# Adaptive-norm block: pairs formed through PSUM, the gate for four chunks at once, more fillers at the end, second norm's statistics on VectorE

## What is computed

```python
h = layernorm(x) * (1 + ca) + sa            # ca, sa, ga, ...: per batch element, from c
q, v = relu(h @ enc_q), relu(h @ enc_v)      # 8 heads of 16
for each head:
    dist = sqrt(sum_e m * (q[window] - q)**2 + 1e-8)   # the 64 tokens up to this one
    keep the 32 nearest of the 64; infl = exp(-dist), normalised
    context = sum over the kept of infl * v
    gate = |q| > 0.2
    out = q * (context + gate * 0.1 * (q / |q|) @ (hebb_U @ hebb_V))
x = x + ga * (out @ decoder)
h = layernorm(x) * (1 + cb) + sb             # the second norm
x = x + gb * (h + routed experts(h))         # expert gates from token 0
```

## Time and profile before

| | |
|---|---|
| three runs | 719.01, 722.64, 726.97 us, median 722.64 |
| profiled execution | 718.8 us, its span 717.0 us |
| mean granted TensorE clock | 0.947 |
| busy: PE, DVE, ACT, POOL | 616.5, 645.2, 559.8, 510.4 us |

### The profile page before, as it was taken

The page is one execution under the profiler, slowest core; times in us unless marked ns, Lnnn a source line. Parts: engine busy times, 40 slices in busy tenths (PEclk is TensorE's granted clock), DMA queues, the critical chain, the costliest instruction groups (busy, mean ns, idle before and its releaser), DMA issues. The chain is left out here.

```text
span 717.0 us, 22533 instructions
## 1 busy us (share of the span) xinstructions
PE 616.5 (86%) x6006; PEld 435.1 (61%) x6069; DVE 645.2 (90%) x4890; ACT 559.8 (78%) x1734; POOL 510.4 (71%) x813
## 2 busy tenths in 40 slices
PE   4987889888889888888888888899888888888776
PEld 3544446666666666666666666666666666666554
DVE  5884698999999999999999999999999999999930
ACT  2895145888888888888888888888888888888753
POOL 3011437888888888888888888888888888888651
PEclk9996587999999999999999999999999999999965
DMA  6320000000000000000000000000000000000000
GB/s 203 88 61 4 10 16 18 21 26 25 26 21 26 23 26 25 26 25 25 26 26 25 25 26 25 22 26 23 25 25 27 25 26 25 26 24 24 16 5 16
DMA packets 41183, 21.22 MB, mean 30 GB/s; under 512 B 6040, under 2 KB 40544, under 8 KB 41056
## 3 DMA queue, kind: packets, MB, share of 16 engines
q1 hardware_dynamic: 41056, 19.77, 9.7%
HBM read 10.44 MB, written 4.19 MB: 20 GB/s over the span
## 5 line engine op out<-in xcount | busy, mean ns | idle before, releaser
L989 DVE MAX8 top<-modn_all 128x8 f32<-128x32 f32 x2048 | 201.7, 175 | 0.0
L558 POOL TENSOR_TENSOR big<-big,con 128x512 f32<-128x512 f32 x128 | 160.0, 1272 | 26.7 <-DVE big L1041 26.7
L995 DVE MATCH_REPLACE8 modn_all<-top,modn_all 128x32 f32<-128x32 f32 x1024 | 166.5, 174 | 0.0
L1218 PE MATMUL psC<-vst,big 128*128 128x68 f32 x512 | 105.1, 288 | 47.8 <-POOL big L558 47.8
L1218 PEld LDWEIGHTS psC<-vst,big 128*128 128x128 f32 x512 | 80.1, 197 | 70.6 <-POOL big L558 70.1
L1219 PE MATMUL psC<-vst,big 128*128 128x68 f32 x512 | 101.7, 281 | 0.0
L1219 PEld LDWEIGHTS psC<-vst,big 128*128 128x128 f32 x512 | 80.6, 199 | 0.0
L995 DVE MATCH_VALUE_LOAD modn_all<-top,modn_all 128x8 f32 x1024 | 77.9, 76 | 0.0
L499 POOL TENSOR_TENSOR wmod_sb<-key,meet 128x512 f32<-128x512 f32 x64 | 67.9, 1062 | 7.4 <-PE psX L1174 7.4
L544 POOL TENSOR_TENSOR t<-cst,rden 128x128 f32<-128x128 f32 x64 | 25.8, 403 | 63.8 <-DVE rden L1030 63.8
L700 ACT ACTIVATE cst<-psC 64x136 f32<-64x136 f32 x128 | 35.6, 278 | 38.3 <-PE psC L1219 36.8
(11 more groups left out here) (214 smaller groups left out, 1630.7 us busy)
## 6 DMA issues: line engine op xcount, KB each, us to landing
tst<-qT_all SPq DMA_DIRECT2D x256, 17.0 KB
big<-in_x SPq DMA_DIRECT2D x16, 256.0 KB, 2.8
xs<-in_x SPq DMA_DIRECT2D x64, 64.0 KB, 1.9
out<-yo SPq DMA_DIRECT2D x64, 64.0 KB, 1.6
sst<-nst SPq DMA_DIRECT2D x128, 3.0 KB
tst<-nst SPq DMA_DIRECT2D x128, 2.0 KB
con<-in_consts SPq DMA_DIRECT2D x1, 581.5 KB, 6.0
wmod_sb<-in_wmod SPq DMA_DIRECT2D x1, 384.0 KB, 4.6
```

The lines of the kernel that those rows point to most:

```text
L558: nc.gpsimd.tensor_tensor(wab[:, k % 2, v].rearrange("p (r t) -> p r t", r=4), wsel.rearrange("p (r t) -> p r t", r=4), part.unsqueeze(1). ...
L989: last = v.max(top[:, u, h, where], low_high[:, u, h])
L995: last = v.match_replace(low_high[:, u, h], top[:, u, h, 1:9], low_high[:, u, h], GONE)
L1218: mm(o, wab[:, k % 2, 0, cols], vst[:, blk + 1:blk + 3, r], start=True, stop=False)
```

## The change

Four edits. (1) The two reductions go. ScalarE writes the upper half of `key`, negated, into free columns of `psD` (`pHi`), and VectorE forms both halves of the pairs by scalar_tensor_tensor from `key` and `pHi` (`pairs`), for chunk i+1 at the end of step i, ahead of the scan. `pHigh` is written by ScalarE too. (2) The mean and variance of the second norm come from bn_stats and bn_aggr on VectorE; what ScalarE still does of it stands at the head of the next step. (3) `lnn`, `rnn`, `gat` and `hsc` are formed for four chunks at once, in every fourth step. (4) The counts of the fillers depend on the step in the last seven, and `drained` adds some in `psD` there. The diff, cut to its core (left out: allocations, semaphores, the indexing of `n2`, and the renumbering of `mix_step`), 8 columns to the left:

```diff
@@ -226,6 +225,7 @@
...
 pQH = pH[:, :, QH0:B0]
+pHi = pH[:, :, PW:PW + HW]
@@ -521,32 +524,33 @@
...
-        k = i + 1
-        if there(k):
-            pool.wait_ge(n2_ready, k + 1)
-            need(pool, mix_step, 4 * (k - 4) + 1)
-            nc.gpsimd.tensor_scalar(gat[:, k % 4], n2[:, k % 4], GATE2, 0.1, ALU.is_gt, ALU.mult).then_inc(gat_ready, 1)
+        if there(i - 2) and i % 4 == 2:
+            four = (i - 2) // 4
+            pool.wait_ge(n2_ready, 4 * four + 4)
+            need(pool, hsc_ready, four)
+            nc.gpsimd.tensor_scalar(gat[:], n2[:, four % 2], GATE2, 0.1, ALU.is_gt, ALU.mult).then_inc(gat_ready, 1)
+            pool.wait_ge(gat_ready, four + 1)
+            pool.wait_ge(rnn_ready, four + 1)
+            need(pool, mix_step, 3 * (i - 2))
+            nc.gpsimd.tensor_tensor(hsc[:], gat[:], rnn[:], ALU.mult).then_inc(hsc_ready, 1)
...
-            pool.wait_ge(rnn_ready, k + 1)
-            pool.wait_ge(gat_ready, k + 1)
-            need(pool, mix_step, 4 * k)
-            nc.gpsimd.tensor_tensor(hsc[:], gat[:, s4], rnn[:, s], ALU.mult).then_inc(mix_step, 1)
-            pool.wait_ge(mix_step, 4 * k + 1)
-            nc.gpsimd.tensor_tensor(t2[:].rearrange(h3, h=NH), hb, hsc[:].unsqueeze(2).broadcast_to([P, NH, HD]),
-                                    ALU.mult).then_inc(mix_step, 1)
+            pool.wait_ge(hsc_ready, k // 4 + 1)
+            need(pool, mix_step, 3 * k)
+            nc.gpsimd.tensor_tensor(t2[:].rearrange(h3, h=NH), hb, hsc[:, k % 4 * NH:(k % 4 + 1) * NH].unsqueeze(2)
+                                    .broadcast_to([P, NH, HD]), ALU.mult).then_inc(mix_step, 1)
@@ -672,18 +676,30 @@
...
-        k = i - 1
-        if there(k):
-            act.wait_ge(n2_ready, k + 1)
-            need(act, mix_step, 4 * (k - 2) + 1)
-            need(act, rnn_ready, k)
-            nc.scalar.activation(lnn[:], n2[:, k % 4], ACT.Ln, bias=bias[:, 6:7]).then_inc(lnn_done, 1)
-            act.wait_ge(lnn_done, k + 1)
-            nc.scalar.activation(rnn[:, k % 2], lnn[:], ACT.Exp, scale=-0.5).then_inc(rnn_ready, 1)
+        k = i - 4
+        if there(k):
+            s = k % 2
+            act.wait_ge(mvc_ready, k + 1)
+            need(act, nc_ready, k - 1)
+            need(act, rs_done, k)
+            nc.scalar.activation(lv_c[:], mv_c[:, s, 1:2], ACT.Ln, bias=bias[:, 0:1]).then_inc(lnc_done, 1)
+            nc.scalar.activation(nm_c[:, s:s + 1], mv_c[:, s, 0:1], ACT.Copy, scale=-1.0).then_inc(nm_done, 1)
+            act.wait_ge(lnc_done, k + 1)
+            nc.scalar.activation(rs_c[:, s:s + 1], lv_c[:], ACT.Exp, scale=-0.5).then_inc(rs_done, 1)
+
+        if there(i - 2) and i % 4 == 2:
+            four = (i - 2) // 4
+            act.wait_ge(n2_ready, 4 * four + 4)
+            need(act, rnn_ready, four)
+            nc.scalar.activation(lnn[:], n2[:, four % 2], ACT.Ln, bias=bias[:, 6:7]).then_inc(lnn_done, 1)
+            act.wait_ge(lnn_done, four + 1)
+            need(act, hsc_ready, four)
+            nc.scalar.activation(rnn[:], lnn[:], ACT.Exp, scale=-0.5).then_inc(rnn_ready, 1)
 
         k = i + 1
         if there(k):
             act.wait_ge(dist_ready, k + 1)
+            need(act, pair_done, 2 * k)
@@ -741,23 +758,18 @@
...
-            need(act, rs_done, k)
-            nc.scalar.activation(x2[:, s], pAtt, ACT.Copy, accum_out=sum_c[:]).then_inc(x2_ready, 1)
-            act.wait_ge(x2_ready, k + 1)
-            nc.scalar.activation(nm_c[:, s:s + 1], sum_c[:], ACT.Copy, scale=-1.0 / D).then_inc(nm_done, 1)
-            act.wait_ge(nm_done, k + 1)
-            nc.scalar.activation(dev_c[:], x2[:, s], ACT.Square, bias=nm_c[:, s:s + 1],
-                                 accum_out=ssq_c[:]).then_inc(ssq_done, 1)
-            act.wait_ge(ssq_done, k + 1)
-            nc.scalar.activation(lv_c[:], ssq_c[:], ACT.Ln, bias=bias[:, 0:1], scale=1.0 / D).then_inc(lnc_done, 1)
-            act.wait_ge(lnc_done, k + 1)
-            nc.scalar.activation(rs_c[:, s:s + 1], lv_c[:], ACT.Exp, scale=-0.5).then_inc(rs_done, 1)
+            nc.scalar.activation(x2[:, k % 2], pAtt, ACT.Copy).then_inc(x2_ready, 1)
...
         k = i + 1
         if there(k):
+            act.wait_ge(d2_ready, k + 1)
+            act.wait_ge(dist_ready, min(k + 2, NCH))
+            need(act, pair_done, 2 * k)
+            high = key[:, k % 2].rearrange("p (h u j) -> p h u j", h=NH, u=2)[:, :, 1]
+            nc.scalar.activation(pHi, high, ACT.Copy, scale=-1.0).then_inc(hi_ready, 1)
+
             e = infl[:, k % 2]
@@ -766,6 +778,14 @@
...
+
+        if there(i):
+            act.wait_ge(picked, 6 * i + 6)
+            need(act, w_ready, i)
+            if i == 0:
+                act.wait_ge(top_set, 2)
+            nc.scalar.activation(pHigh, top[:, 1].rearrange("p h n -> p (h n)"), ACT.Copy,
+                                 scale=-1.0).then_inc(high_done, 1)
@@ -995,14 +1015,21 @@
...
+    def pairs(k):
+
+        lo = key[:, k % 2].rearrange("p (h u j) -> p h u j", h=NH, u=2)[:, :, 0]
+        dve.wait_ge(hi_ready, k + 1)
+        need(dve, picked, 6 * k - 1)
+        v.scalar_tensor_tensor(out=low_high[:, 0], in0=pHi, scalar=-1.0, in1=lo, op0=ALU.mult,
+                               op1=ALU.min).then_inc(pair_done, 1)
+        need(dve, picked, 6 * k)
+        v.scalar_tensor_tensor(out=low_high[:, 1], in0=lo, scalar=-1.0, in1=pHi, op0=ALU.mult,
+                               op1=ALU.min).then_inc(pair_done, 1)
+
     def step(i):
         if there(i):
-            x4 = key[:, i % 2].rearrange("p (h u j) -> p h j u", h=NH, u=2)
-            dve.wait_ge(d2_ready, i + 1)
+            dve.wait_ge(pair_done, 2 * i + 1)
             need(dve, theta_ready, i)
-            v.tensor_reduce(low_high[:, 0], x4, AX_X, ALU.min).then_inc(pair_done, 1)
-            v.tensor_reduce(low_high[:, 1], x4, AX_X, ALU.max, negate=True).then_inc(pair_done, 1)
-            dve.wait_ge(pair_done, 2 * i + 1)
@@ -1045,16 +1072,25 @@
...
+        k = i - 3
+        if there(k):
+            dve.wait_ge(x2_ready, k + 1)
+            need(dve, mvc_ready, k)
+            v.bn_stats(st_c[:], x2[:, k % 2]).then_inc(stc_ready, 1)
+
         if there(i):
             dve.wait_ge(picked, 6 * i + 4)
             pick(1, 1)
 
+        if there(k):
+            dve.wait_ge(stc_ready, k + 1)
+            need(dve, nc_ready, k - 1)
+            v.bn_aggr(mv_c[:, k % 2], st_c[:]).then_inc(mvc_ready, 1)
+
+        if there(i + 1):
+            pairs(i + 1)
+
         if there(i):
-            dve.wait_ge(picked, 6 * i + 6)
-            need(dve, w_ready, i)
-            if i == 0:
-                dve.wait_ge(top_set, 2)
-            v.tensor_scalar(pHigh, top[:, 1].rearrange("p h n -> p (h n)"), -1.0, None, ALU.mult).then_inc(high_done, 1)
             dve.wait_ge(high_done, i + 1)
             need(dve, diff_ready, i - 1)
             v.tensor_tensor_scan(meet[:, i % 2].rearrange("p h n -> p (h n)"), pHigh,
@@ -1202,6 +1238,12 @@
...
+    def drained(times):
+
+        if times:
+            pe.wait_ge(pair_done, 2 * NCH)
+            keep_clock(psD[:, 0], PW, times)
...
             need(pe, cst_ready, 2 * k)
-            keep_clock(psC, PW, 3)
+            keep_clock(psC, PW, {NCH: 0, NCH + 1: 9}.get(i, 3))
...
+        drained({NCH - 1: 3, NCH: 3}.get(i, 0))
...
+        drained({NCH + 2: 2, NCH + 3: 6}.get(i, 0))
...
+            keep_clock(psX, PW, {NCH - 3: 3, NCH - 2: 4, NCH - 1: 3}.get(i, 0))
...
+        drained({NCH + 2: 3, NCH + 3: 2}.get(i, 0))
...
-            keep_clock(psX[:, 2 * P:4 * P], P, 2)
+            keep_clock(psX[:, 2 * P:4 * P], P, {NCH - 2: 6, NCH - 1: 5, NCH: 3, NCH + 1: 7}.get(i, 2))
```

32 lines of the change are left out of this document (17 added, 15 removed).

## The result

The changed kernel takes 686.73 us (median of 4 runs, 686.03 to 695.29), the kernel before in the same comparison 720.83 (4 runs, 718.79 to 726.97). The ratio is 0.954, 95% interval 0.944 to 0.964. The profiled execution has a span of 685.2 us against 717.0.

A forecast was written before the change was run, and what follows sets the result against it. VectorE, busy 90% of the span, was taken as the bound, its 9.29 us step falling to 8.75. Span 717.0 + 7.5 (head) - 34.2 (62 steps) - 7 (tail) = 683.3 us, so 689 us as median; range 676 to 706.

The forecast's parts named there:

- head: The first steps, up to scan 1, get longer because the pairs wait for pHi: +7.5 us, bounds +5 and +10.
- tail: From the last scan to the end, 45 more filler matmuls keep TensorE's clock: -7 us, bounds -9.5 and 0.
- VectorE's row: VectorE's own work in a step: 9.29 - 1.21 - 0.34 + 0.67 + 0.29 = 8.70 us.
- an idle of 0 to 0.1 before the scan: Sign on VectorE in the middle of the run: it waits only that long, in us, for ScalarE's pHigh.
- The loop: Two steps, from W through transposes, Ln, Exp, pHigh and scan back to a W: 8.72 us a step.
- the gate's delay: On ScalarE in every fourth step, lnn and its Exp: at most 0.6 us, 0.15 a step, taken as 0.03.
- the next step is shorter by VectorE's own: The step from scan 0 to scan 1 shrinks by 0.9 us, so scan 1 comes 7.5 later, not 8.4.
- the rival that it falls: TensorE's clock falls in the tail despite the new fillers: +10, 699 us; chance 0.14.
- Everything fits: Rival: 8.65 us a step, head +5, tail -9, giving 678 us; chance 0.09.
- The loop of 9.0: Rival: ScalarE comes 0.5 late to pHigh, once in two steps, so 9.0 us a step: 704 us; chance 0.12.
- the clock in the middle of the run: Rival: TensorE's clock falls there too, each such step costing 11.3 us, 766 us if in half; chance 0.03.
- pairs that wait: Rival: on VectorE the pairs wait 0.54 us for ScalarE in each step, giving 722 us; chance 0.02.

The follow-up runs named there:

- e3: The changed kernel with the two reductions of before in place of the pairs, and no pHi on ScalarE; 699.17 us.
- e10: e7 with the gate's Ln and Exp for four chunks moved on ScalarE to behind x2 of the step before; 668.51 us.
- e2: The changed kernel with pHigh negated on VectorE again, ahead of the scan; 690.96 us.
- e8: The changed kernel with three unread one-column copies on ScalarE between the last picks and pHigh; 702.06 us.
- e5: The changed kernel with the gate of before, 8 columns wide in each step on ScalarE and GpSimd; 696.75 us.
- e7: The changed kernel with pHigh between the influences' Ln and Exp on ScalarE, not behind the Exp; 672.18 us.
- e4: The changed kernel with the second norm's statistics on ScalarE as before, bn_stats and bn_aggr gone; 706.38 us.
- e9: The changed kernel with pHigh(0) ahead of pHi(1) on ScalarE and scan 0 ahead of the pairs of chunk 1 on VectorE; 685.42 us.
- e11: e10 without the fillers that the change added in steps 61 and 62; those from step 63 on stay; 668.55 us.
- e6: The changed kernel with one and one filler matmuls in place of three and two in steps 6 to 60; 686.16 us.

## Why the prediction was right, and where it was not

The time was right, 689 forecast and 686.7 measured, and so were the three parts of the sum: head +7.5 forecast and +6.8 measured (with a start 1.8 earlier), 62 steps -34.2 and -31.8, tail -7 and -6.8. The reasons are right in part. The head's number owes something to chance: counted from the distances of chunk 1 it costs 8.6, and the earlier start hides 1.8 of it.

**VectorE's row** was mis-sized: 8.70 forecast, 8.46 in e3 and e10, 8.48 in e2. Two of its terms are too high. The statistics were put at 0.29; they cost 0.16. The sixteen picks behind W took 1.61 (416.60 to 418.21), and picks and statistics together now take 1.77 (404.17 to 405.94): the picks are two times eight, of 0.75, and bn_stats stands between them, where 1.61 - 2 x 0.75 = 0.11 used to be idle. The pairs were put at 0.67 and take 0.64. Most of the rest, 0.08, lies between `den` and the instruction behind it, which forms the second half of `key`: some 0.25 before and 0.19 now. So VectorE idles 8.73 - 8.46 = 0.27 a step for pHigh, and the sign "an idle of 0 to 0.1 before the scan" was missed.

**The loop** had the right length, 8.72 for 8.73, and the wrong course. The step "(11.91 + 5.53) / 2" closes it through W and VectorE over two steps. The chain that the runs show has one step, and doesn't pass through W: Ln, Exp, pHigh, scan, GpSimd's difference, `key`, `cst`, `fst`, the counts, the distances, the transposes, Ln. The prediction names most of them, but not `cst`, `fst` and the counts, which close it. It set the gate's delay to almost nothing "since the relu behind them has to wait for GpSimd's difference in any case": that wait is 0.18, and the gate is 0.47, so 0.28 of it shows. A delay of ScalarE ahead of `fst` is paid in each step and not in every second one: e8 shows it, 0.25 a step where two steps would give 0.14, and e5 and e7 fit; e4's 9.055 fits both loops. That both loops give the same number is chance. One term stands in no row of the kernel before: Ln 0.05 behind the transposes, where those rows have 417.03 and 417.20. The changed kernel has 0.05 (405.41, 405.46).

**Where the negations stand.** The Trainium skill (ScalarE: Activation LUTs, Rules for kernel authors) would keep them on VectorE. Measured, pHigh on ScalarE behind the Exp gains 0.07 a step (e2 against the change), ahead of the Exp 0.28 (e2 against e7's mean of 8.52). The rows spoke against the rule and were right for pHigh (the place of pHi was not varied alone); more than the engine, it is the place in its queue that counts.

**The pairs never wait,** as forecast, in the usual steps: L1023 and L1026 last 0.39 and 0.41. The cover is smaller than the 1.1 forecast: pHi ends 1.8 after W (405.38), 0.56 ahead of the pairs. The wait of 0.78 ahead of C went to 0.2 and 0, as forecast.

**The head.** The products start 2.6 after the distances of chunk 1 (forecast 2.5), take 1.2 each, and the expert matmuls come 1.9 later than before, counted the same way (forecast 2.4). Scan 0 came at 105.13 + 1.8 = 106.9 (forecast 106.8). The step that failed is "the next step is shorter by VectorE's own": it took 12.21 as before (12.18), with 1.28 of wait for pHigh. Two things hold scan 0: pHigh(0), and the pairs of chunk 1 ahead of it, which need pHi(1). Both stand on ScalarE behind `nst`, which waits 10.6 for matmuls that TensorE does behind the expert products. Counted from the distances of chunk 1, scan 1 comes 31.6 later; without pHi (e3) it is 29.1, with pHigh on VectorE (e2) 30.0, with pHigh ahead of the Exp (e7) 29.6, in the order of e9 30.1. So each takes 1.5 to 2.6 of the 8.6 away, while the other hold stays; e3's 2.6 contain the 1.9 of the expert matmuls, which start 3.2 after the distances there, as in the kernel before. No run lifts both holds, so that the other 6 hang on them is argued from the rows and not shown.

**The tail.** The clock holds, the rival that it falls is refuted. But the prediction's -7 is not what the fillers are worth. Without them the tail is 28.4 and not 30.35, and the last scan comes 1.7 to 2.9 earlier. The fillers' own part is -2 to -3, too little for the medians. The prediction costed them as standing in waits; in steps 61 to 63 they stand in TensorE's row. That -7 and -6.8 agree is chance too.

**The rivals.** "Everything fits" (8.65 a step) falls for this kernel, and e10 at 8.46 shows that only ScalarE's order stood in its way. The loop of 9.0, the clock in the middle of the run, and pairs that wait are refuted by the rows above.

## What to carry to other kernels

Ask of a loop not only how long it is but how many steps it spans, and test it: put a known delay on one member and see whether each step pays all of it or half; measure the delay in the trace of that run, since mine was half of what I had planned. When an engine is no longer the bound, its small instructions can go where another engine's queue has a gap: the same two instructions of the gate cost 0.28 us in their step ahead of what TensorE waits for (0.35 in e7) and nothing in front of a wait (e10). Fillers that hold a clock belong where the engine waits; in a full row they cost time, here 1.2 us for those of two steps (e11 against e10).

## What the runs showed of the hardware that I had not expected

The time at which the clock comes back after the first steps is not a property of the kernel. The changed kernel and e6 are the same program up to step 5, but steps 2 and 3 took 10.23 and 8.52 in the one and 13.22 and 13.49 in the other. Windows of the changed kernel, then of e6:

```profile
125.00:145.00 20.00, 17.99 (x210) 12.49 (x197) 18.97 (x164) 15.57 (x44) 16.50 (x21) 1.00 0.07 19
```

```profile
125.00:145.00 20.00, 19.34 (x142) 12.80 (x144) 12.02 (x93) 9.78 (x27) 9.29 (x11) 0.57 0.05 13
```

At the granted clock of 0.57 two steps cost 8 us more (the step before them took 1.0 less). The single runs of 695.29 (changed), 693.5 (e6), 676.69 (e11) and 679.61 (e7) have the lowest mean clocks of their kernels (0.943 to 0.951), so this is likely much of the spread that hides 1 us; only the profiled ones among them (e6, e11) show the slow steps. The start differs too: the distances of chunk 1 began at 85.38 in e10 and at 89.28 in e11, with the same program ahead of them.

The two products of 1024 elements took 2.73 us each beside GpSimd's own and take 1.2 alone (2.35 for both, above); in e3, where they stand beside GpSimd's again, they take 2.03 each. GpSimd's two took 4.73 beside them, in the kernel before and in e3, and 3.75 in the changed kernel. Also, L1003 with 512 elements took 1.13 while GpSimd's L502 ran (105.72, 1.06 long) and 0.69 otherwise. The Trainium skill (SBUF — State Buffer, SBUF: two separate sides) has a VectorE instruction with two SBUF inputs and a GpSimd one that reads SBUF exclude each other; these rows agree with it in kind, though no run here varied that alone.

An Exp that reads what the Ln ahead of it wrote starts 0.72 after it (405.46 to 406.18). With pHigh between them it starts 0.80 after it, so that an instruction of 0.21 costs 0.08 there (387.03 to 387.83). bn_stats between the two groups of picks on VectorE looks like the same effect: the groups take 1.61 without it (416.60 to 418.21) and 1.69 with it (404.17 to 405.86), where bn_stats holds VectorE for 0.19.
